# Two weight matrices turned by VectorE instead of TensorE, in a four-layer conditional residual block

## The reference

```
x = x + x @ W.T + scal[a] * (x @ A[a].T) @ Bm[a].T     # a = idx0 of the sequence: its low-rank adapter, of 8
x = x + w1[b].T @ x                                     # b = idx1: a 64x64 mixing over tokens, of 200
q, k, v = x @ Wq.T, x @ Wk.T, x @ Wv.T                  # 16 heads of 32
p = softmax(causal(min(cond, 4) * q @ k.T / sqrt(32)))
x = x + heads(p @ v) @ Wo.T
x = x + w3[c].T @ x                                     # c = idx3: a 64x64 mixing over tokens, of 8
```

## Time and profile before

| | |
|---|---|
| median of 3 runs | 619.65 us (619.6 to 620.12) |
| profiled execution, its own time | 619.72 us |
| its span, first to last instruction | 618.0 us |
| TensorE busy | 604.5 us, 98% of the span |
| VectorE, ScalarE, GpSimd busy | 386.8, 225.0, 109.7 us |
| mean granted TensorE clock | 0.997 |

### The profile page before, as it was taken

How to read it: one execution, slowest core, us unless ns; L and a number is a source line. 1 busy time by engine, 2 the same in 40 slices (tenths; PEclk the granted TensorE clock), 3 DMA queues, 4 the chain that set the end, 5 groups by cost and what they waited for, 6 DMA issues and landing times.

```text
span 618.0 us, 21481 instructions
## 1 busy us (share of the span) xinstructions
PE 604.5 (98%) x8534; PEld 522.7 (85%) x8534; DVE 386.8 (63%) x561; ACT 225.0 (36%) x434; POOL 109.7 (18%) x101
## 2 busy tenths in 40 slices
PE   6999999899999999999999999999999999999998
PEld 5897979789898888989888898988989788898885
DVE  3569676565766756576675757666575765637374
ACT  4534533242434425143342514435152442413222
POOL 2004030120303003030310303021030302203030
PEclk9999999899999999999999999999999999999999
DMA  8541313222232222223222222323223222220212
GB/s 276 168 146 48 90 43 83 73 50 70 72 88 72 60 72 63 72 76 93 68 64 72 62 74 72 76 74 79 72 57 79 72 64 73 60 73 5 69 41 103
DMA packets 62104, 48.29 MB, mean 78 GB/s; under 512 B 16826, under 2 KB 47546, under 8 KB 62074
## 3 DMA queue, kind: packets, MB, share of 16 engines
q1 hardware_dynamic: 58122, 41.84, 24.9%
q10 hardware_dynamic: 3952, 6.03, 2.9%
HBM read 30.54 MB, written 17.30 MB: 77 GB/s over the span
## 4 chain that ended last, share of the span: by engine, by line
PE 95%; DVE 1%; DMA 1%; issue 1%; ACT 1%; ACTq 0%; DVEq 0%
PE banks L617 10%; PE banks L622 10%; PE banks L618 10%; PE banks L645 5%; PE banks L716 5%; PE banks L717 5%; PE banks L723 5%; PE banks L647 5%; PE banks L649 5%; PE banks L557 5%; PE banks L559 5%; PE banks L561 5%; PE banks L670 4%; PE banks L662 4%; PE banks L686 3%; PE banks L601 3%
## 5 line engine op out<-in xcount | busy, mean ns | idle before, releaser
L617 PE MATMUL banks<-x1T_hi,w_hi 128*128 128x256 f32 x512 | 130.3, 287 | 0.2 <-ACT x_in L885 0.2
L618 PE MATMUL banks<-x1T_hi,w_lo 128*128 128x256 f32 x512 | 128.2, 283 | 0.0
L617 PEld LDWEIGHTS banks<-x1T_hi,w_hi 128*128 128x128 f32 x512 | 98.0, 191 | 0.8 <-ACT x_in L885 0.4
L618 PEld LDWEIGHTS banks<-x1T_hi,w_lo 128*128 128x128 f32 x512 | 98.1, 192 | 0.0
L1374 POOL TENSOR_TENSOR probs<-probs,row_max 128x1024 f32<-128x1024 f32 x32 | 61.0, 1906 | 123.5 <-DVE row_max L1176 123.5
L622 PE MATMUL banks<-x1T_lo,w_hi 128*128 128x256 f32 x512 | 82.2, 283 | 0.0
L1356 POOL TENSOR_TENSOR w_own<-w_in,own 128x128 f32<-128x128 f32 x32 | 14.7, 460 | 361.4 <-PE banks L584 267.4
L622 PEld LDWEIGHTS banks<-x1T_lo,w_hi 128*128 128x128 f32 x512 | 70.6, 192 | 0.0
L1162 DVE TENSOR_TENSOR qkT<-banks,beta 128x512 f32<-128x512 f32 x32 | 22.1, 690 | 61.7 <-PE banks L622 61.7
L885 ACT ACTIVATE x_y<-banks 128x512 f32<-128x512 f32 (+1 forms) x17 | 9.9, 584 | 128.8 <-PE banks L584 122.0
L1180 DVE TENSOR_REDUCE row_sum<-probs 128x16 f32<-128x1024 f32 x32 | 39.0, 1218 | 24.2 <-ACT probs L966 24.2
(11 more groups left out here) (133 smaller groups left out, 1055.3 us busy)
## 6 DMA issues: line engine op xcount, KB each, us to landing
x_rows<-x_in SPq DMA_DIRECT2D x64, 128.0 KB, 2.3
x_kept<-x_rows SPq DMA_DIRECT2D x16, 512.0 KB, 3.7
x_in<-in_x_dram SPq DMA_DIRECT2D x60, 128.0 KB, 2.8
out_dram<-x_y SPq DMA_DIRECT2D x15, 512.0 KB, 3.0
b_sel<-b_parts SPq DMA_DIRECT2D x180, 32.0 KB, 1.7
w_in<-in_L_cond_weights_dram SPq DMA_DIRECT2D x128, 16.0 KB
probsT<-in_L_cond_W_dram ACTq DMA_DIRECT2D x1, 1024.0 KB, 7.3
probs<-in_L_cond_Wk_dram ACTq DMA_DIRECT2D x1, 1024.0 KB, 5.9
```

What stands on the lines that cost most here:

```text
L617: nc.tensor.matmul(out_ap, w_hi[:, w, c, cols], x1T_hi[:, c, :], start=(c == 0), stop=False)
L618: nc.tensor.matmul(out_ap, w_lo[:, w, c, cols], x1T_hi[:, c, :], start=False, stop=False)
```

## The change

WV and WO are no longer turned by TensorE. Each is loaded in blocks by four DMAs of 256 KB (`load_blocks`), to 32 partitions each, in runs of 512 bytes. VectorE turns a part of 128 output columns at a time with its block transpose into a new buffer `w_whole` of four parts (`turn_w`); ScalarE copies a part as hi (`part_hi`) and VectorE computes lo (`part_lo`). Parts 0 to 3 are WV, parts 4 to 7 WO. WV's load is issued earlier, behind the eviction of W, and WO's behind the copies of WV's first three parts. Three of WV's parts are turned between the groups of WK, the fourth after the tables; WO's parts 4 and 5 around the scaling of the first queries, parts 6 and 7 in step 0.

In step 0 the first query part is put ahead of the key parts, with the wait for the split of x1 in it. A block transpose of contiguous runs gives WO's chunks other rows than TensorE's turn did, so attention writes its heads in the matching order: products of one chunk j run over m, and head JG*m + j lands in rows of group m instead of j.

```diff
+        w_whole = sb("w_whole", [P, NC, NC, P])
...
-                 WV: as_stage(probsT[:], "p t (c d) -> p (t c) d"),
-                 WO: x2_y[:].rearrange("p a t d -> p (a t) d")}
+                 WV: probsT[:].rearrange("p t n -> p (t n)").rearrange("p (b n) -> p b n", n=P),
+                 WO: x2_y[:].rearrange("p a t d -> p (a t d)").rearrange("p (b n) -> p b n", n=P)}
...
+        PARTS_V, PARTS_O = range(NC), range(NC, 2 * NC)
+        def matrix_part(w, n):
+            k = WV if n in PARTS_V else WO
+            return w[:, k, :, n % NC * P:(n % NC + 1) * P]
+        def whole_part(n):
+            return w_whole[:, n % NC]
...
# TensorE: attention (attend_last alike)
-                    for m in range(NC):
+                    for j in range(JG):
                         for r in range(SEQT):
-                            for j in range(JG):
+                            for m in range(NC):
...
-                                    attn_bank(r)[j * HD:(j + 1) * HD, m, t, :], v[half(r), t, head:head + HD],
+                                    attn_bank(r)[m * HD:(m + 1) * HD, j, t, :], v[half(r), t, head:head + HD],
...
# TensorE: step
+                if not prev:
+                    pe.wait_ge(part_split, len(PARTS_V))
                 values(i, 0)
...
                     adapters_down(2)
-                    turn_part(WO, 0)
+                pe.wait_ge(x1_hi_done, TILES * (i + 2))
+                if not prev:
+                    query_part(0, split=TILES * 2)
                 pe.wait_ge(x1_copied, SEQT * i + 1)
-                pe.wait_ge(x1_hi_done, TILES * (i + 2))
                 for m in range(NC):
...
                     key_part(i + 1, m)
-                    if not prev and m > 0:
-                        if m == 1:
-                            pT_copied(0, HG)
-                        turn_part(WO, m)
-                if not prev:
-                    pe.wait_ge(turned_lo, GROUPS_OF[WO][0] + 1)
-                for m in range(NC):
+                for m in range(NC) if prev else range(1, NC):
...
-                    pe.wait_ge(turned_lo, GROUPS_OF[WO][-1] + 1)
+                    pe.wait_ge(part_split, len(PARTS_V) + len(PARTS_O))
                 scores(i + 1)
...
# TensorE: prelude
-            turn_part(WV, 0)
             pe.wait_ge(x1_hi_done, TILES)
             for m in range(NC):
                 key_part(0, m)
-                if m == 0:
-                    pe.wait_ge(tables_done, PSEQ)
-                else:
-                    turn_part(WV, m)
+            pe.wait_ge(tables_done, PSEQ)
...
# ScalarE
+            def load_blocks(k, matrix):
+                for g in range(JG):
+                    act.dma_start(stage[k][g * SQ:(g + 1) * SQ],
+                                  matrix.rearrange("(b j) (g n) -> g j b n", j=SQ, g=JG)[g]).then_inc(w_loaded[k], 16)
+            def part_hi(n):
+                act.wait_ge(part_turned, n + 1)
+                copy(matrix_part(w_hi, n), whole_part(n)).then_inc(part_hi_done, 1)
...
# ScalarE: step 0, behind xa_low_part(2)
-                    take_hi(GROUPS_OF[WO][0], w_hi[:, WO, 0, :])
+                    xa_hi_part(2)
+                    for n in PARTS_O[1:]:
+                        part_hi(n)
                     copy_k(1)
-                    for c in range(1, NC):
-                        take_hi(GROUPS_OF[WO][c], w_hi[:, WO, c, :])
-                    xa_hi_part(2)
...
# ScalarE: prelude
             take_matrix(W0)
+            load_blocks(WV, Wv)
             take_hi(GROUP_A, a_all[:, 0:2, :], in_chunks(bank_of_group(GROUP_A))[:, 0:2, :])
...
-            load_w(WV, Wv)
             for c in range(3):
                 take_hi(GROUPS_OF[WK][c], w_hi[:, WK, c, :])
+                part_hi(c)
+            act.wait_ge(xa_first_split, 1)
+            load_blocks(WO, Wo)
             x0_copy(0)
...
             take_hi(GROUPS_OF[WQ][3], w_hi[:, WQ, 3, :])
-            load_w(WO, Wo)
-            take_hi(GROUPS_OF[WV][0], w_hi[:, WV, 0, :])
+            part_hi(3)
             x_hi(1)
-            take_hi(GROUPS_OF[WV][1], w_hi[:, WV, 1, :])
             copy_k(0)
-            for c in (2, 3):
-                take_hi(GROUPS_OF[WV][c], w_hi[:, WV, c, :])
...
             select_a(1)
+            part_hi(PARTS_O[0])
             xa_low_part(1)
...
# VectorE
+            def turn_w(n):
+                k, first = (WV, PARTS_V[0]) if n in PARTS_V else (WO, PARTS_O[0])
+                if n == first:
+                    dve.wait_ge(w_loaded[k], 16 * JG)
+                if k == WO:
+                    dve.wait_ge(part_split, n - NC + 1)
+                blocks = stage[k][:, NC * (n - first):NC * (n - first + 1), :]
+                nc.vector.transpose(
+                    whole_part(n).rearrange("p c (b j) -> p b c j", j=SQ),
+                    blocks.rearrange("p b (e c) -> p b c e" if k == WV else "p b (c e) -> p b c e", c=NC))\
+                    .then_inc(part_turned, 1)
+            def part_lo(n):
+                dve.wait_ge(part_hi_done, n + 1)
+                rest(matrix_part(w_lo, n), whole_part(n), matrix_part(w_hi, n)).then_inc(part_split, 1)
...
# VectorE: step 0, behind scale_xa(2)
-                    for c in range(NC):
-                        if c == NC - 1:
-                            copy_k(1)
-                        take_lo(GROUPS_OF[WO][c], w_lo[:, WO, c, :], w_hi[:, WO, c, :])
+                    for n in PARTS_O[2:]:
+                        turn_w(n)
+                    for n in PARTS_O[1:]:
+                        part_lo(n)
+                    copy_k(1)
...
# VectorE: prelude
             for c in range(3):
                 take_lo(GROUPS_OF[WK][c], w_lo[:, WK, c, :], w_hi[:, WK, c, :])
+                turn_w(c)
             x0_copy(0)
...
-            take_lo(GROUPS_OF[WV][0], w_lo[:, WV, 0, :], w_hi[:, WV, 0, :])
+            turn_w(3)
             turn_x(1)
-            for c in (1, 2):
-                take_lo(GROUPS_OF[WV][c], w_lo[:, WV, c, :], w_hi[:, WV, c, :])
+            for n in PARTS_V:
+                part_lo(n)
             copy_k(0)
-            take_lo(GROUPS_OF[WV][3], w_lo[:, WV, 3, :], w_hi[:, WV, 3, :])
             x_lo(1)
+            turn_w(PARTS_O[0])
             scale_q(0)
+            turn_w(PARTS_O[1])
+            part_lo(PARTS_O[0])
             sum_xa(1)
```

More of the change, by code:

```diff
@@ L196, in cond_resid_kernel @@
         tables_done = sem("tables_done")
+        part_turned = sem("part_turned")
+        part_hi_done = sem("part_hi_done")
+        part_split = sem("part_split")
         xT_mm = sem("xT_mm")
@@ L257, in cond_resid_kernel @@
         GROUP_A, GROUP_B = 4, 5
-        GROUPS_OF = {W0: range(0, 4), WK: range(6, 10), WQ: range(10, 14), WV: range(14, 18), WO: range(18, 22)}
-        ring = [0, 6, 7, 4, 5, 6, 7, 4, 5, 6, 0, 7, 6, 7, 6, 7, 6, 7, 0, 5, 6, 7]
+        GROUPS_OF = {W0: range(0, 4), WK: range(6, 10), WQ: range(10, 14)}
+        ring = [0, 6, 7, 4, 5, 6, 7, 4, 5, 6, 0, 7, 6, 7]
         XA_FIRST, ROWS = 0, 1
@@ L285, in attn_of @@
         def attn_of(ap, r):
-            return ap.rearrange("p m (t b s) -> p b m t s", t=TILES, b=SEQT)[:, r]
+            return ap.rearrange("p j (t b s) -> p b j t s", t=TILES, b=SEQT)[:, r]
         def attn_bank(r):
-            return bank[AT[r]].rearrange("p (m t s) -> p m t s", m=NC, t=TILES)
+            return bank[AT[r]].rearrange("p (j t s) -> p j t s", j=NC, t=TILES)
         def own_blocks(r):
@@ L324, in last_attn @@
         def last_attn(ap, t, r):
[L325 removed]
+            return ap.rearrange("p j (t b s) -> p j t b s", t=TILES, b=SEQT)[:, :, t, r]
         def last_attn_bank(t, r):
[L328 removed]
+            return bank[SC[TILES * t + r]][:, 0:PT].rearrange("p (j s) -> p j s", j=NC)
         HALF_D = D // 2
+        PARTS_V, PARTS_O = range(NC), range(NC, 2 * NC)
[4 more added lines that the diff above has]
+            return w_whole[:, n % NC]
         block = ctx.enter_context(nc.Block())
@@ L489, in pieces_of @@
             def pieces_of(k, dc):
-                if k != WO:
-                    return [every_fourth(stage[k][:, oc, :], dc) for oc in range(NC)]
-                return [stage[k][:, oc, dc * P:(dc + 1) * P] for oc in range(NC)]
+                return [every_fourth(stage[k][:, oc, :], dc) for oc in range(NC)]
             def turn_part(k, dc):
@@ L629, in key_part, with query_part @@
                     last.then_inc(k_mm, 1)
-            def query_part(m):
-                last = project_T(WQ, Q, m)
+            def query_part(m, split=None):
+                last = project_T(WQ, Q, m, split)
                 if m % 2 == 1:
@@ L698, in attend_last @@
                                 last = nc.tensor.matmul(
-                                    last_attn_bank(t, r)[j * HD:(j + 1) * HD, m, :], v[half(r), t, head:head + HD],
+                                    last_attn_bank(t, r)[m * HD:(m + 1) * HD, j, :], v[half(r), t, head:head + HD],
```

1 line of the change is left out of this document (removed).

## The result

The changed kernel takes 631.11 us (median of 4 runs, 628.51 to 631.83) against 619.62 us: 1.0189 times as long, 95% interval 1.0165 to 1.0213. A second set of 6 runs gave 627.86 us (624.30 to 632.62), 1.0144 (1.0106 to 1.0182). The forecast was 623.1 with a range of 619.5 to 625.9: slower, as forecast, but by 8 to 11.5 us for the 3.5 of the forecast. The profiled execution is the first set's fastest, 628.51 us with a span of 626.8, 8.8 more than before.

The account below looks back on a forecast made before the run. TensorE, busy 98% of the span, was taken to bound the kernel. The terms +5.1 + 1.3 - 1.9 - 1.0 = +3.5 on 619.72 us gave 623.2, as a median 623.1, with a range of 619.5 to 625.9.

Parts of the forecast that it names:

- the lockstep and the issues: Ahead of step 0: alternating waits of ScalarE and VectorE, plus WO's four load issues, delay x0's copy; TensorE 5.1 us late.
- the slow clock: Behind that pause ahead of step 0: TensorE at half clock for 3.4 us, costing 1.3 us, bounds 0 and 1.7.
- WV's turns on TensorE: Ahead of step 0: four groups of WV no longer turned by TensorE, 0.48 us each, 1.9 us saved.
- VectorE's uncovered copy of k: Step 0: TensorE waits 0.69 us plus hand-overs for this copy behind the last key part, until 70.0.
- x1 was turned: Step 0: VectorE's added turn and split make the turns of x1 0.7 us later.
- -1.0 at the end: End of step 0: WO's splits are done earlier, so the second scaling of q starts 1.0 us earlier.
- WO's turns: VectorE's turns of WO from contiguous runs: 0.9 us each, taken from 0.76 to 1.12.
- Late blocks: Rival, ahead of step 0: WV lands near 22, each microsecond past 20.9 is added, 624 to 625 us; chance 0.08.
- The other side: the pause at 114.40 goes.: Rival, first loop pass: TensorE's 1.98 us pause and its slow stretch vanish, 3.7 us saved, 619.4 us; chance 0.15.

Follow-up runs that it names:

- no_lockstep: Changed kernel with ScalarE's copies of WV's parts out of the loop over WK's parts and WO's load issues behind WQ's last part: 623.07 us (1.0058).
- turns_late: Changed kernel with WV's four turns and ScalarE's copies of them behind WQ's last part, and WO's four load issues there too: 621.39 us (1.0055).
- fill64: Changed kernel with 64 more TensorE instructions, 16 small products in its wait for W0's diagonal: 624.92 us (1.0095).
- after_again: The changed kernel itself, unaltered, run again for a second profile: 627.86 us (1.0144).

## Why the prediction was right in sign and too small

**The prelude: right, term by term, in this profile.** +5.1 for the lockstep and the issues: the pause is 5.07, and the mixing products begin 5.3 late (31.07 against 25.73). +1.3 for the slow clock: from there to the first key part it took 5.37, and 3.92 in no_lockstep and turns_late, at full clock, so 1.45. -1.9 for WV's turns on TensorE: the first of the four stood ahead of that key part, about 0.5, and the other three make 6.4 (36.44 against 30.07) into 4.8 at the first scores, -1.6. WV's turns took 1.10 us each against 1.12. That the slow clock came so near its term has luck in it: the stretch was twice as long as the 3.4 us taken from before, and nearly half of it lay in the pause. In fill64 and after_again it lay later, the same way took 6.30 and 6.23, and the slow clock cost 2.3 to 2.4, more than the forecast's bound of 1.7. The window of fill64, where the mixing products begin at 31.18:

```profile
30.20:37.00 6.80, 6.21 (x27) 4.41 (x28) 3.86 (x6) 4.14 (x8) 0.00 (x0) 0.50 1.02 160
```

**Step 0: right in its sum.** TensorE waited 0.78 for VectorE's uncovered copy of k, to 74.38; the text had 70.0 on the clock of before, so 74.8 with the 4.8 of the prelude. One step on the way was not so: x1 was turned at 63.09, which is 58.32 on the clock of before, not 0.7 late. -1.0 at the end: 4.8 had become 3.7, -1.1. Sum without the pauses: +3.7 against +3.5. fill64, in which one pause stands as before, measured +5.4 (its profile +5.2), of which about 1.0 is the longer slow clock ahead of its first key part (37.48 against 36.44); its own products cost 0.1 by the mixing.

**WO's turns: too dear.** 0.70 us from contiguous runs, not 0.9. The Trainium skill's "Vector Engine (DVE) Microarchitecture Reference", section 3.8, with its element per cycle, would give about 0.7, an estimate from the page, and so agrees with this row; for the strided WV the measured 1.10 decides against it. It changed nothing in the time.

**Late blocks: the place was right, the landing too early.** From 15 to 21 us the queues moved 183 to 189 GB/s, not 239. The blocks land just in time here, not at 18.6, and 0.3 and 0.6 late in other profiles of the same prelude. Where TensorE's first product began 3.3 later they cost 4.85. The upper end of the range, 625.9, is not the sum that is named for it (623.1 + 2 = 625.1); the measured times lie above both.

**The step that failed: "The other side: the pause at 114.40 goes."** It saw that the pause might hang on the place in the stream, gave that 0.15, and then priced only this one pause, staying or going, and going as a gain. The pause is one visible case of 21 block ends. Moving the stream by 64 instructions moves them all; that of the loop's first pass stayed at instruction 2753 and only met other products, and two more ends came to lie in dense ones. The sum had no term for new pauses and put them at nothing without a reason. What the runs put in its place: about 4.6 us of the profile's 8.8 (8.8 less fill64's 5.2, and the 1.0 by which fill64's slow clock cost more), and between the medians of the two sets and fill64's 2.9 and 6.2. "Against it: nothing shows that the place matters" was wrong: q8 on the page, 21 packets of 16 KB, and the pause in the first pass alone were to be read together, and the distance from it to each dense stretch counted.

## What to carry to other kernels

Where TensorE pauses in the midst of equal small products, count its instructions up to the pause and look for an instruction packet; an edit that adds or removes instructions ahead moves every such pause, and can be slower or faster for that alone, so compare versions at equal block ends (a fill of small products does it; 16 cost about 0.1 us inside a wait here, 48 cost 2.8) before judging the edit. Two engines that alternate waits for each other pay the sum of their durations, however idle each looks; put the one's copies behind the work that the path needs. A load that "just arrives" is a bound, not a zero.

## What the hardware showed unexpectedly

192 more instructions on TensorE in the kernel before cost 8.8 us, three times the 2.8 that they take themselves. A block was usable about 3.3 us after the one before was entered in the common case, but 5.0 in step 0 and 5.8 at the last pause; in both cases its packet began just behind a burst of 0.5 MB of data traffic (81.8, and near 613). turns_late, with 0.02 MB there in step 0, had its packet after 0.9 us; but before_fill192, with 0.06 MB, had it after 2.5. So whether a burst holds the packet up stays open. An instruction of two waits that are already met takes TensorE about 0.11 us. VectorE turns 512 elements a lane in 0.70 us from contiguous runs in SBUF and in 1.10 us with a stride of four. With a pause of 5 us came 6.8 us at half the clock, beginning 2 us into it, in the changed kernel; pauses of 1 to 2.7 us were followed by 3.4 us at half the clock or by none. In the kernel before, of 60 executions on three chips, 31 have a mean clock of 1.000 and took 617.3 to 618.9 us, and 28 have 0.997 and took 619.5 to 620.7: one slow stretch, there in about half of them, costs 2.0 us.
